# A two-stack windowed-attention kernel: the values product moved behind the transposes, SyncE's copies swapped, one sine operation per q or k, and the normalisations of the middle stage moved to VectorE

## What is computed

```python
def _layer(x, wqkv, qs, ksc, wo, lg, lb, w1, b1, w2, b2):
    h = shift_token(x)
    q, k, v = split(h @ wqkv)                 # 8 heads of 64
    q = l2norm(q) * qs;  k = l2norm(k) * ksc
    q, k = rotary_xpos(q, k)                  # q*cos*scale + rotate_half(q)*sin*scale
    o = local_attention(q, k, v)              # windows of 64, own and previous window
    x = x + o @ wo
    h = layernorm(shift_token(x)) * lg + lb
    a, g = split(h @ w1 + b1)                 # 341 columns each
    return x + (a * gelu(g)) @ w2 + b2

x = x + 0.5 * stack(layernorm(x))             # stack = two layers
y = layernorm(x)
k, q, v = (layernorm(y @ W + b) * g + beta for W in (Wk, Wq, Wv))
x = x + y + softmax(k @ q.T) @ v              # full attention over 1024 tokens
x = x + 0.5 * stack(layernorm(x))
```

## Time and profile before

| | |
|---|---|
| median of 3 runs | 1809.63 us (1808.24 to 1811.32) |
| the profiled execution's own time | 1811.45 us |
| its span, first to last instruction | 1809.7 us |
| mean granted TensorE clock | 0.967 of full speed |
| busy, share of the span | PE 84%, DVE 73%, ACT 65%, POOL 61% |
| the chain that ended last | PE 51%, DVE 26%, ACT 9%, issue 7%, SPq 3%, DMA 2%, POOL 1% |

### The profile page before, as it was taken

How to read it: one execution, slowest core, us unless ns; L and a number is a source line. 1 busy time by engine, 2 the same in 40 slices (tenths; PEclk the granted TensorE clock), 3 DMA queues, 4 the chain that set the end, 5 groups by cost and what they waited for, 6 DMA issues and landing times.

```text
span 1809.7 us, 44041 instructions
## 1 busy us (share of the span) xinstructions
PE 1523.7 (84%) x15864; PEld 1237.8 (68%) x15864; DVE 1323.5 (73%) x3420; ACT 1174.8 (65%) x2460; POOL 1098.1 (61%) x1130
## 2 busy tenths in 40 slices
PE   1789999978999999867878979999998899999984
PEld 1677777766777777754656757777776777777763
DVE  6687879777788887754434469797977687979772
ACT  1576767666677776745565567676766576767671
POOL 3685858576677676633232168585857576858560
PEclk9999999999999999988889989999999999999996
DMA  8241212231312131113100142122223131212113
GB/s 282 49 123 39 59 46 57 55 86 45 77 42 57 40 80 40 41 50 97 35 12 24 33 104 53 44 53 50 55 58 89 41 77 41 58 47 54 44 28 118
DMA packets 183670, 112.46 MB, mean 62 GB/s; under 512 B 86720, under 2 KB 164128, under 8 KB 182944
## 3 DMA queue, kind: packets, MB, share of 16 engines
q1 hardware_dynamic: 183456, 109.65, 23.2%
HBM read 43.41 MB, written 23.42 MB: 37 GB/s over the span
## 4 chain that ended last, share of the span: by engine, by line
PE 51%; DVE 26%; ACT 9%; issue 7%; SPq 3%; DMA 2%; POOL 1%; DVEq 0%; ACTq 0%; POOLq 0%
PE QK L388 10%; PE TO L638 9%; PE QK L638 5%; PE TO L705 5%; DVE rope_c L1136 5%; DVE rope_s L1141 4%; DVE o_n L1161 4%; PE TO L388 3%; DVE top L1080 3%; PE SC L679 3%; DVE h2n L1148 3%; PE TO L807 2%; PE VB L807 2%; PE TO L751 2%; ACT probs L1278 2%
## 5 line engine op out<-in xcount | busy, mean ns | idle before, releaser
L1278 ACT ACTIVATE probs<-SC,shift,qgain 128x128 f32<-128x128 f32 x1024 | 389.7, 480 | 102.2 <-DVE shift L1088 101.9
L1472 POOL TENSOR_TENSOR ve<-mv,epsilon 128x1 f32<-128x1 f32 x128 | 24.3, 190 | 393.4 <-DVE mv L1127 393.4
L388 PE MATMUL QK<-w_qkv,hT 128*128 128x512 f32 x768 | 223.7, 429 | 23.4 <-DMA w_qkv<-qkv_d 10.9
L1136 DVE TENSOR_TENSOR rope_c<-QK,rope 128x512 f32<-128x512 f32 x256 | 175.7, 686 | 81.5 <-PE QK L388 79.0
L1485 POOL TENSOR_TENSOR rnorm<-clip,mhalf 128x8 f32<-128x8 f32 x128 | 210.9, 1647 | 13.1 <-DVE clip L1097 13.1
L1494 POOL TENSOR_TENSOR qgain<-clip,mhalf 128x8 f32<-128x8 f32 x128 | 209.3, 1635 | 0.0
L638 PE MATMUL TO<-ident,probs 128*128 128x128 f32 x1280 | 188.7, 274 | 20.8 <-ACT probs L1278 11.2
L1272 ACT ACTIVATE v_own<-VB 128x512 f32<-128x512 f32 x128 | 76.5, 598 | 191.1 <-PE VB L388 191.1
L1080 DVE TENSOR_REDUCE top<-SC 128x4 f32<-128x512 f32 x256 | 174.6, 682 | 28.8 <-PE SC L679 28.5
L1141 DVE TENSOR_TENSOR rope_s<-QK,rope 128x256 f32<-128x256 f32 x512 | 190.9, 415 | 0.0
L638 PEld LDWEIGHTS TO<-ident,probs 128*128 128x128 f32 x1280 | 152.4, 141 | 54.8 <-issue 34.3
(11 more groups left out here) (170 smaller groups left out, 3760.8 us busy)
## 6 DMA issues: line engine op xcount, KB each, us to landing
v_prev<-v_own SPq DMA_DIRECT2D x256, 130.0 KB, 2.3
x_att<-stream SPq DMA_DIRECT2D x128, 64.0 KB, 2.3
h<-stream SPq DMA_DIRECT2D x256, 32.0 KB, 1.9
stream<-x_new SPq DMA_DIRECT2D x32, 256.0 KB
w_qkv<-qkv_d SPq DMA_DIRECT2D x3, 1536.0 KB, 6.8
h<-x_mid SPq DMA_DIRECT2D x128, 32.0 KB
h<-x_mid SPq DMA_DIRECT2D x128, 31.8 KB
rope<-rope_d SPq DMA_DIRECT2D x24, 128.0 KB, 3.2
```

What stands on the lines that cost most here:

```text
L388: last = mm(dst, fr(left(a)), fr(right(b)), start=(k == 0), stop=(k == 2))
L1136: v.tensor_tensor(qk(rope_c[:])[:, m], src, rope[:, i, m, 0:1, :].to_broadcast([P, HEADS, DH]), ALU.mult)
L1278: last = nc.scalar.activation(probs[:, b, hd, :], SC[:, hd * P:hd * P + P], ACT.Exp, bias=shift[:, b, hd:hd + 1], scale=qgain[:, b, hd % 4 ...
```

## The change

Four things.

1. TensorE's values product stands behind the transposes of h and h2n and ahead of the transposes of o_n. The two transposes go to the first 256 columns of `TT` instead of `VB`. So the transposes of the probabilities of half 0 in the next step, which write there, wait for `s_hl` and `s_h2l`. ScalarE's copy of v stands behind its copies of hT and h2T and ahead of that of oT, and VectorE's `norm` behind its two subtractions. In a burst the first product waits for `s_h2l` and `s_hl` for the same reason.
2. SyncE issues the copies to `h2` ahead of those to `v_prev`.
3. The sine part of the rotation is one VectorE operation of 512 columns for q and one for k, in place of two of 256 each; the halves are read through a reversed view.
4. In the middle stage VectorE normalises y, k and q (`tensor_scalar`: subtract the mean, multiply), ScalarE only v and the output. For y, k and q GpSimd works out only the power. The last piece of `prepared(g, 5)` stands behind the row's maximum.

```diff
                     if t := tile(ATT):
+                        if t2 := tile(TH + 1):
+                            pe.wait_ge(s_hl, t2.count())
+                        if t2 := tile(FFN_IN + 1):
+                            pe.wait_ge(s_h2l, t2.count())
                         probs_transposed(t, 0)
...
-                        product(mm, VB[:], lambda x: hT[:, b, x, :], lambda x: w_qkv[:, x, 1024:1536]).then_inc(s_v, 1)
...
-                        transpose(VB[:, 0:P], h[:, t.i % 4, :]).then_inc(s_th, 1)
+                        transpose(TT[:, 0:P], h[:, t.i % 4, :]).then_inc(s_th, 1)
...
-                        transpose(VB[:, P:2 * P], h2n[:, t.i % 2, :]).then_inc(s_th2, 1)
+                        need(pe, s_h2l, t.count(back=1))
+                        transpose(TT[:, P:2 * P], h2n[:, t.i % 2, :]).then_inc(s_th2, 1)
+                    if t := tile(QKV):
+                        b = t.i % 2
+                        need(pe, s_vown, t.count(back=1))
+                        if before is not None:
+                            pe.wait_ge(s_xn, before * 2 + 1)
+                        product(mm, VB[:], lambda x: hT[:, b, x, :], lambda x: w_qkv[:, x, 1024:1536]).then_inc(s_v, 1)
...
-                        sin = rope[:, i, m, 1:2, :]
-                        for half in range(2):
-                            a, o = 32 * half, 32 * (1 - half)
-                            last = v.tensor_tensor(qk(rope_s[:])[:, m, :, a:a + 32], src[:, :, o:o + 32],
-                                                   sin[:, :, a:a + 32].to_broadcast([P, HEADS, 32]), ALU.mult)
+                        sin = rope[:, i, m, 1:2, :].rearrange("p o (a d) -> p o a d", a=2)
+                        last = v.tensor_tensor(qk(rope_s[:])[:, m].rearrange("p h (a d) -> p h a d", a=2),
+                                               src.rearrange("p h (a d) -> p h a d", a=2)[:, :, ::-1, :],
+                                               sin.to_broadcast([P, HEADS, 2, 32]), ALU.mult)
...
+                if (s := prepared(g, 1)) is not None:
+                    y_normalised(s)
+                if (s := prepared(g, 5)) is not None:
+                    shifted_in(s, 7)
+                    z_stats(s, 6)
+                    z_stats(s, 7)
+                    z_moments(s)
...
+            def z_normalised(s, m):
+                dve.wait_ge(g_rsk, s * 4 + (2 * m + 2))
+                zz = z_n(s)[:, :, m * DIM:m * DIM + DIM]
+                normalise(zz, zz, KQV + m * TILES).then_inc(g_zn, 1)
```

More of the change, by code:

```diff
@@ L785, in w1_pair @@
                         pe.wait_ge(s_act2, n * 6 + (k - 1))
+                    if k == 0:
+                        pe.wait_ge(s_h2l, last_in.count())
+                        if t := tile(TH):
+                            pe.wait_ge(s_hl, t.count())
                     if k == 1 and n == ITERS - 1:
@@ L800, in w2_half @@
                     if half == 0:
-                        if t := tile(TH):
-                            pe.wait_ge(s_hl, t.count())
+                        if t := tile(QKV):
+                            pe.wait_ge(s_vown, t.count())
                     elif t := tile(ATT):
@@ L1166, in step @@
                     shifted(t, 1)
-                if t := tile(QKV):
-                    b = t.i % 2
-                    dve.wait_ge(s_sq, t.count())
-                    need(dve, s_rn, t.count(back=2))
-                    v.tensor_reduce(norm2[:, b, :], sq[:].rearrange("p (h d) -> p h d", d=DH), AX, ALU.add).then_inc(s_n2, 1)
                 if t := tile(TH):
@@ L1181, in step @@
                     own = slice(t.i * P, t.i * P + P)
-                    v.tensor_tensor(fr(h2T[:, 1, own]), VB[:, P:2 * P], h2T[:, 0, own], ALU.subtract).then_inc(s_h2l, 1)
+                    v.tensor_tensor(fr(h2T[:, 1, own]), TT[:, P:2 * P], h2T[:, 0, own], ALU.subtract).then_inc(s_h2l, 1)
+                if t := tile(QKV):
+                    b = t.i % 2
+                    dve.wait_ge(s_sq, t.count())
+                    need(dve, s_rn, t.count(back=2))
+                    v.tensor_reduce(norm2[:, b, :], sq[:].rearrange("p (h d) -> p h d", d=DH), AX, ALU.add).then_inc(s_n2, 1)
                 if burst == ITERS - 1:
@@ L1244, in _ @@
                     v.reciprocal(rl_g[:, b:b + 1], sm_g[:, b:b + 1]).then_inc(g_rl, 1)
+                if (s := prepared(g, 6)) is not None:
+                    z_normalised(s, 0)
                 if t := row(g - 2):
@@ L1260, in _ @@
                         aggregate(LN_OUT).then_inc(g_mvo, 1)
+                if (s := prepared(g, 6)) is not None:
+                    z_normalised(s, 1)
             pipeline(step, 1)
@@ L1317, in step @@
                     need(act, s_v, t.count(back=2))
-                    copy(fr(hT[:, t.i % 2, 0, :]), VB[:, 0:P]).then_inc(s_hT, 1)
+                    copy(fr(hT[:, t.i % 2, 0, :]), TT[:, 0:P]).then_inc(s_hT, 1)
                 if t := tile(FFN_IN):
                     act.wait_ge(s_th2, t.count())
-                    copy(fr(h2T[:, 0, t.i * P:t.i * P + P]), VB[:, P:2 * P]).then_inc(s_h2T, 1)
+                    copy(fr(h2T[:, 0, t.i * P:t.i * P + P]), TT[:, P:2 * P]).then_inc(s_h2T, 1)
+                if t := tile(QKV):
+                    b = t.i % 2
+                    act.wait_ge(s_v, t.count())
+                    need(act, s_o, t.count(back=TILES - 1))
+                    if t.c >= 2:
+                        act.wait_ge(s_vlo[b], t.count(back=2, every=2, unit=16))
+                        act.wait_ge(s_vup[b], t.count(back=2, every=2, unit=16))
+                    copy(v_own[:, t.i, :].rearrange("p (h d) -> p h d", h=HEADS)[:, :, 0:DH],
+                         VB[:].rearrange("p (h d) -> p h d", h=HEADS)).then_inc(s_vown, 1)
                 if t := tile(ATT):
@@ L1538, in after @@
                 if g == DRAIN + 4:
-                    for m in range(3):
-                        rstd_and_shift(KQV + m * TILES, m + 1, g_mvk, g_rsk, g_nbk)
+                    kqv_rstd(0)
             pipeline(step, 0, after)
```

117 lines of the change are left out of this document (50 added, 67 removed).

## The result

| | before | after |
|---|---|---|
| median of 13 runs | 1810.05 us (1805.35 to 1814.53) | 1816.37 us (1811.22 to 1822.15) |
| ratio | | 1.0035, 95% interval 1.002 to 1.005 |
| profiled execution, span | 1809.7 us | 1811.4 us |
| busy PE, DVE, ACT, POOL | 84%, 73%, 65%, 61% | 85%, 76%, 63%, 60% |
| chain, share of PE, DVE, ACT | 51%, 26%, 9% | 40%, 34%, 6% |

The change makes the kernel 6 us slower, where the forecast was 1798, 12 us faster. The time is inside the forecast range, but on the other side of no change.

The account below looks back on a forecast made before the run. The prediction took a loop through several engines, none full, as the bound. 1811.45 + 18 (stacks) - 30 (middle), with the runs' median 1.8 below the profiled execution, gave 1798 us; its own range was 1785 to 1812, the full range 1765 to 1825.

Parts of the forecast that it names:

- the stacks' term: All steps outside the middle stage: 112 steps, each 0.16 us longer, +18 us.
- The plain step: Step without a burst: shift1 held until q_r ends, then subtractions and TT's wait; about 9.32 instead of 9.16 us.
- there are 16 iterations of 6, plus 16 steps with a burst whose opening is alike: 112: Count of steps in the stacks that were each to lose 0.16 us, giving +18 us.
- The burst's opening: First product of a burst waits for s_h2l and s_hl as in a plain step: the same 0.16 us.
- The middle, -30: Middle stage: VectorE's shorter normalisations and earlier row maxima save 18 in z, 10 in y, 2 in the first sequence.
- The saving is not on the loop: Sine operation in the rotation: 0.13 us a step saved, hidden by 2.6 us of slack ahead of q_r.
- the bad end: Reversed sine view read at half the pace: 1.1 us a step more, mostly hidden, at most 0.1 a step, +11.
- SyncE's order at 0, covered: h2 copies issued about 2 us earlier cover the late copy of v: 0; without cover mv late one for one.
- A: Rival, chance 0.15: shift1 slips in ahead of q_r in the plain step; time about 1740, or 1708 us.
- B: Rival, chance 0.15: the wait on TT is covered, plain steps stay 9.1 to 9.18; 1780 or down to 1772 us.
- A's two prices: Plain step with shift1 ahead of q_r: 8.75 us if GpSimd holds the clip until k_a ends, 8.41 if free.
- C: Rival, chance 0.15: another engine limits the middle stage, which gives only 8; 1819 us, deciding if it gives under 18.

Follow-up runs that it names:

- experiment 2: The stacks' changes alone (values product and waits, SyncE's order, sine) on the kernel before, middle stage as before: 1841.84 us, ratio 1.0169.
- experiment 1: The middle stage's normalisations and order alone, on the kernel before: 1784.26 us, ratio 0.9846.
- experiment 3: The changed kernel with VectorE's two subtractions moved ahead of the shift of half 1: 1767.15 us, ratio 0.9752 to the kernel before.
- experiment 9: The changed kernel with VectorE's norm ahead of the two subtractions, as before the change: 1969.29 us, ratio 1.0883 to the kernel before.
- experiment 6: The changed kernel with the second layer's weights loaded earlier and the w_qkv load split in two: 1788.31 us, ratio 0.9871 to the kernel before.
- experiment 4: The changed kernel with GpSimd's values of the first sequence behind VectorE's y normalisation of the second: 1812.19 us, ratio 1.0008 to the kernel before.
- experiment 5: The single sine operation of 512 columns alone, on the kernel before: 1795.93 us, ratio 0.9925.
- experiment 8: The changed kernel with two sine operations of 256 columns again: 1840.53 us, ratio 1.0162 to the kernel before.
- experiment 7: The changed kernel with SyncE's old order, copies to v_prev ahead of those to h2: 2185.26 us, ratio 1.2065 to the kernel before.
- experiment 11: The kernel before with the sine and middle-stage changes, GpSimd's values behind y, and second-layer loads one step earlier: 1750.08 us, ratio 0.9666.
- experiment 10: The changed kernel with experiment 3, experiment 4 and experiment 6 together: 1731.57 us, ratio 0.9565 to the kernel before.

## Why the prediction was wrong

The sum was 18 lost in the stacks and 30 won in the middle. Measured between the `mv`s: 30 and 25; as runs of their own, 31 and 27 (experiments 2 and 1). Both terms were of the right sign, and the difference between them was not. The larger miss is the stacks' term. That the time fell inside the forecast range is no merit of the sum.

- *The plain step*: right. 9.35 for 9.33, with each point on the way: shift1 at 5.82 behind `mv` (5.85), the hT subtraction at 7.00 (7.00), the half-0 transposes at 7.58 (7.53), the output product at 8.04 (8.02), oT over at 7.16 (7.2 to 7.4). Experiments 3 and 9 move the two operations that it names and get 8.80 and 10.47.
- *"there are 16 iterations of 6, plus 16 steps with a burst whose opening is alike: 112"*: this step failed. It put +18 for the stacks, and the stacks lose 29.6. Plain steps gave 0.18 each, 10.6 for the 60 that are plain all through. The largest part of what was missing stands where I had counted more plain steps: at the change of layer two loads hang on the values product and on ScalarE's copy of v, by a semaphore and by a place in SyncE's list. I followed the two moved things to their waits in the plain step, and not in the queue they stand in once per stack: +9.2, 7.2 of it in the waits for the loads. Experiment 6 shows that the long steps there are the loads'; taking them off the path wins more than the change had added. The steps behind a burst, which I left out, cost 0.13 and 0.28.
- *The burst's opening "as a plain step does, so I give it the same 0.16"*: right for ten of the twelve bursts of the table, which take 23.97 in the mean for 23.83. The other two take 25.51, 3.1 of the row's 4.8. TensorE used to go straight into a burst, and `s_h2l` was wanted three pairs later; now it stands idle for up to 1.67 there, and in these two the granted clock fell behind it (below). The forecast had no term for the clock.
- *The middle, -30*: mis-sized, -24.6. The two sequences in full swing gave -11.9 and -9.9 for a forecast of -11 each. The first was forecast at -6 for its rows and was +4.3: the y normalisation held for 4.2 (experiment 4), which I should have seen, as the prediction itself rests on GpSimd holding VectorE's operations of this kind, and yet priced them at the one free row without asking what GpSimd does then. The stretch ahead of the rows gave -4.6 (forecast -2), that from the fourth sequence's rows on -2.6 (0).
- *"The saving is not on the loop"* of the sine: wrong. It is worth 14 in the old order and 24 in the new one (experiments 5 and 8). In the old order the rotation and the held `h2n` are on the chain of the 9.19 steps themselves; I had looked at the slack of q_r alone. In the new order the hold goes over ScalarE, a way I had not followed. The sum was not hurt, since it took `h2n` as free, but the price stood in the wrong part, and "at most 0.1 a step" for the bad end would have been too small: experiment 8, with some 0.13 more of VectorE's time, loses 0.15 a step.
- *SyncE's order at 0, covered*: right, and experiment 7 shows the cover to be worth 370.
- *The rivals*: A and B did not happen in the changed kernel; A's first half, a shift ahead of q_r, was missed as worked out, by 0.03. A's open question, whether GpSimd holds a clip, is answered in the first step behind the burst at the change of layer, where one meets q_r and takes 1.11 for 0.17:

```profile
476.61 1.27 POOL L1510 TENSOR_TENSOR q_r<-rope_c,rope_s 128x512 f32<-128x512 f32 x1
476.80 1.11 DVE L1116 TENSOR_SCALAR clip<-norm 128x8 f32<-128x8 f32 x1
```

So of A's two prices the 8.75, which counts on a held clip, had the reason and the 8.41 had not. Experiment 3 comes to 8.80, though there `norm` sets it and the clip of a plain step is not held (0.17). C, the slower one, had the sign and not the mechanism: the middle gave 25, above its threshold of 18, and the stacks took more than that.

## What to carry to other kernels

When an operation is moved later in a step, list everything that waits for it over the whole program, the once-per-layer loads and what merely stands behind a waiter in the same queue. Here the change of layer, twice in the program, lost 9.2, nearly as much as 60 plain steps (10.6). Where two engines hold each other, each newly placed operation has to be laid over the other engine's timeline before it gets a price. And a slot in which the engine is held anyway is the place for short operations of which others wait: two subtractions moved ahead of a held shift turned a loss into 2.5% gained.

## What the runs showed that I had not expected

In the changed kernel two steps with a burst take 25.51 in place of 23.98. In both TensorE's granted clock is 0.93 in the mean of the step, against 1.00 in the others of the table's twelve. The timeline at one of them, and the stretches of 2 us around it (PE, PEld, DVE, ACT, POOL busy, granted clock, DMA share, GB/s):

```profile
254.09 2.54 PE L389 MATMUL TO<-h2T,w 128*128 128x512 f32 x6 [1.67 <-DVE h2T L1197]
```

```profile
252.50:254.50 2.00, 0.41 (x2) 0.40 (x3) 2.00 (x4) 1.98 (x5) 2.00 (x2) 1.00 0.05 15
254.50:256.50 2.00, 2.00 (x7) 1.51 (x6) 0.61 (x1) 1.15 (x2) 0.30 (x1) 0.50 0.51 119
256.50:258.50 2.00, 2.00 (x7) 1.56 (x6) 0.75 (x1) 0.55 (x1) 0.00 (x0) 0.64 0.00 0
```

TensorE stood idle for 1.67 waiting for the h2T subtraction, and behind it the clock was at its half (1.2 of 2.4 GHz) for some 3.4 us (all of the second stretch and 0.64 in the mean of the third); the six matmuls took 2.54 in place of 1.65. In the ten other bursts of the table about the same idle time (1.67 in nine, 1.49 in one) passes without it. I counted such bursts in the profiled executions, without the one at each change of layer: none before, none in experiments 1, 5 and 11 (old order, no wait of the burst's first product); 2 in the changed kernel, 4 in experiment 2, 3 in experiment 4, 5 in experiment 6 (idle 1.67 ahead of nearly all); none in 3 and 10 (idle 0.98); but 6 in experiment 8, where the idle time there is only 0.99, 6 in experiment 9 (idle 2.5 to 2.8) and 11 in experiment 7 (idle 1.2 to 1.7). So the idle time ahead of the burst is not what decides it alone, and the cause stays open. It is worth 1.5 us each time in the changed kernel, and some of the wider spread of the changed kernel's times (11 us over 13 runs, before 9) may be that.
